# A graph network's edge placement: the weight half of each block's payload products moves from VectorE to GpSimd

## The chip, the core and the metric

The kernel runs on one core of one Trainium2 chip. The metric is the device time of one execution in microseconds, the lower the better; a row of the profile is one instruction or one group of instructions of the engines TensorE (PE, its weight loads PEld), VectorE (DVE), ScalarE (ACT), GpSimd (POOL) and SyncE (SP).

## The reference, cut to what matters

Four graph layers follow each other on 3,125 nodes with 128 features and 53,125 directed edges that are sorted by destination: attention (L0), a sum over neighbours (L1), a layer whose messages carry a weight for each edge (L2), and a relational sum (L3). Only what bears on the change is shown.

```python
loop = arange(3125)
src = concatenate([s, d, loop]); dst = concatenate([d, s, loop])   # then sorted by dst
# L2: a weight for each edge, from its four attributes
e_h = silu(edge_attr @ edge_W1 + edge_b1)
e_w = sigmoid(e_h @ edge_W2 + edge_b2)                             # [53125, 1]
x_agg = silu(x[src] @ agg_W + agg_b) * e_w
out = segment_sum(x_agg, dst) / max(count(dst), 1)
# L0, L1 and L3 use src, dst (and L3 the edge's type) in the same way, without e_w
```

## The kernel before

The nodes are cut into NB = 25 blocks of 128. Before the first layer the kernel sorts the edges into slots: for each block b of destinations and each block j of sources (JN = 26 of them, one for what overflows) there is a tile of 128 slots, and all four layers then work tile by tile with one-hot matrices. This sorting is called placement here. It is a loop over the 25 blocks of destinations. The edges stand in 416 columns of 128, and block b owns a window of CW = 20 columns.

For each block VectorE makes, in this order and each as one instruction: `ohj` (the one-hot of an edge's source block, 20 x 26 bf16 in a partition, line 1578), `LO` (the one-hot of its slot, 128 x 20 bf16, line 1580), and two products at line 1584. A product multiplies `ohj` by three values of each edge and fills half of the payload `PAY` (20 x 3 x 26 = 1,560 bf16 in a partition). Half 0 carries three fields (the offsets of source and destination, the type) and half 1 the edge's weight, split into three bf16 parts. At the end of the block VectorE adds up the three weight parts that came back for the block before (`slot_weights`, line 1546, from PSUM into `EWS`). The values stand in `Wp[:, b, half]`: GpSimd copies them out of the columns, the fields for all blocks at line 837 early on, the weights at line 851 when they are there.

TensorE's `place(b)` (line 2319) multiplies the 20 columns of `LO` by those of `PAY` into a PSUM bank, ScalarE copies the result out (lines 1050 and 1051), and `slot_weights(b)` follows. `ohj`, `LO`, `PAY` and the PSUM bank have two buffers each, taken by b % 2, so VectorE may run up to two blocks ahead of `place`.

The weights come from a small network over the edge attributes, which TensorE and ScalarE compute in pieces (`hidden_piece`: lines 2242, 2255 and 2234 on TensorE, 1031 on ScalarE). They come in two halves. The first is complete before the placement, and serves the blocks 0 to 12 (EARLY = 13). The second is made while blocks 0 to 9 are placed (REST = 10): TensorE's queue holds two `hidden_piece` calls around each `place(n)`, n < 10, and the last of them, the sigmoid and the turned columns come after `place(9)`. Then GpSimd splits the second half into its three parts (lines 844 and 847) and copies the windows of the blocks 13 to 24.

The order of each engine's work is that of the code, engine by engine; between engines there are counting semaphores alone. The ones that matter:

```python
dve.wait_ge(win_ew, b + 1)        # VectorE, ahead of both products: the weights of block b are copied
pool.wait_ge(place_done, NB)      # GpSimd, after its copies: nothing to do until the placement ends
pe.wait_ge(pay_ready, b + 1)      # TensorE, ahead of place(b)
```

After block 24 VectorE compares the first rows of the slots (line 1554), and the first layer begins.

Of the kernel before, what the change touches and what calls it, by code (L numbers as in the profile page):

```python
# [8 lines left out]
ALU = mybir.AluOpType  # L9
# [3 lines left out]
P = 128  # L13
# [31 lines left out]
def gnn_kernel(nc, ins, out):  # L45
    N = ins["x"].shape[0]
    E = ins["src"].shape[0]
    NB = -(-N // P)
# [7 lines left out]
    CW = min(20, NCH)  # L56
# [15 lines left out]
    EARLY = max(0, min(NB, (16 * HA - CW - 4) * P * NB // E + 1))  # L72
    REST = SETS - SB
# [132 lines left out]
    with ctx:  # L206
# [3 lines left out]
        def sem(name):  # L210
            return ctx.enter_context(nc.semaphore(name))
# [56 lines left out]
        PJ = JN // 2  # L268
# [4 lines left out]
        Wp = ring[:, 6240:6240 + 2 * PAYS * NBC].rearrange("p (b w c k t) -> p b w c k t", w=2, c=CW, k=3, t=2)  # L273
# [185 lines left out]
        win_cp = sem("win_cp")  # L459
# [20 lines left out]
        rank_mm = sem("rank_mm")  # L480
        rank_done = sem("rank_done")
        pay_ready = sem("pay_ready")
        place_done = sem("place_done")
        slots_cp = sem("slots_cp")
        ews_done = sem("ews_done")
# [161 lines left out]
        def chunk(n):  # L647
            return adj3[:, n % CBUF, :, :] if n % CBUF < 3 else adj3v[:, n % CBUF - 3, :, :]

        def to_widen(eng, s):  # L650
            n = chunk_of(s)
            eng.wait_ge(adj_io[n % CBUF], adj_stored(n % CBUF) + 16 * (n // CBUF + 1))
            eng.wait_ge(applied, NB * BANKS + max(0, s - XBUF + 1))
            q, b = STEPS[s]
            w = even_width(q)
            return adjf[:, s % XBUF, 0:w], chunk(n)[:, b % ACH, 0:w]

        @block.sync
        def _(sp):
# [155 lines left out]
        def _(pool):  # L815
# [22 lines left out]
            pool.wait_ge(attr_tr, 4)  # L838
            G.tensor_copy(IN, iota_i[:, :].unsqueeze(2).to_broadcast([P, P, CW])).then_inc(pool_consts, 1)

            for h in range(2):
                cs = slice(16 * HALF[h][0], 16 * (HALF[h][-1] + 1))
                pool.wait_ge(ew_act, 3 * h + 2)
                G.tensor_tensor(ewr[:, cs], EW[:, cs], ewp[:, 0, cs], ALU.subtract).then_inc(ew_sub, 1)
                pool.wait_ge(ew_act, 3 * h + 3)
                pool.wait_ge(ew_sub, 2 * h + 1)
                G.tensor_tensor(ewp[:, 2, cs], ewr[:, cs], ewp[:, 1, cs], ALU.subtract).then_inc(ew_sub, 1)
                pool.wait_ge(ew_sub, 2 * h + 2)
                for b in (range(0, EARLY), range(EARLY, NB))[h]:
                    at = pool.value_load(cbi[0:1, b:b + 1], min_val=0, max_val=NCH - CW)  # L850
                    G.tensor_copy(Wp[:, b, 1, :, :, :], ewp[:, :, bass.ds(at, CW)].rearrange("p k c -> p c k").unsqueeze(3).to_broadcast([P, CW, 3, 2])).then_inc(win_ew, 1)

            pool.wait_ge(place_done, NB)
            G.memset(vals[:, :, :, ROW0:VW], 1.0).then_inc(ones_col, 1)
# [524 lines left out]
        def _(dve):  # L1379
# [8 lines left out]
            def loose(instr):  # L1388
                done[0] += 1
                instr.then_inc(dve_order, 1)  # L1390
                return done[0]
# [183 lines left out]
            for b in range(NB):  # L1575
                if b >= 2:
                    dve.wait_ge(place_done, b - 1)
                m = loose(V.tensor_tensor(ohj[:, b % 2, :, :].rearrange("p c (h t) -> p c h t", t=2), IJ2.unsqueeze(1).to_broadcast([P, CW, PJ, 2]),
                                          jr2[:, b, :, :].unsqueeze(2).to_broadcast([P, CW, PJ, 2]), ALU.is_equal))
                loose(V.tensor_tensor(LO[:, b % 2, :, :], IN, lo[:, b, :].unsqueeze(1).to_broadcast([P, P, CW]), ALU.is_equal))  # L1580
                dve.wait_ge(dve_order, m)
                dve.wait_ge(win_ew, b + 1)
                for half in range(2):
                    o = V.tensor_tensor(PAY[:, b % 2, :, 3 * half:3 * half + 3, :].rearrange("p c k (h t) -> p c k h t", t=2),  # L1584
                                        ohj[:, b % 2, :, :].rearrange("p c (h t) -> p c h t", t=2).unsqueeze(2).to_broadcast([P, CW, 3, PJ, 2]),
                                        Wp[:, b, half, :, :, :].unsqueeze(3).to_broadcast([P, CW, 3, PJ, 2]), ALU.mult)
                settle()
                o.then_inc(pay_ready, 1)
                if b:
                    slot_weights(b - 1)  # L1590

            dve.wait_ge(pay_ready, NB)
            for h in FIRST:
                for f in range(2):
                    edge_hots(h, f, 0)
# [607 lines left out]
        def _(pe):  # L2203
# [106 lines left out]

            def place(b):
                pe.wait_ge(pay_ready, b + 1)
                if b >= 2:
                    pe.wait_ge(slots_cp, b - 1)
                    pe.wait_ge(ews_done, b - 1)
                else:
                    pe.wait_ge(rank_done, NB)
                for c in range(CW):
                    o = T.matmul(bank(5 + b % 2)[:, 0:PAYS * JN], LO[:, b % 2, :, c],  # L2319
                                 PAY[:, b % 2, c, :, :].rearrange("p k j -> p (k j)"), start=c == 0, stop=c == CW - 1)  # L2320
                o.then_inc(place_done, 1)
# [429 lines left out]
```

## Time and profile before

| | before |
|---|---|
| median of 3 runs | 1109.53 us (1106.13 to 1110.77) |
| span of the profiled execution | 1106.8 us, 2.7 us under the median |
| placement, from the first `ohj` to the last product | 102.4 to 202.1 us of that span |
| VectorE busy in the placement | 93.73 of 99.80 us |
| TensorE busy in the placement | 85.69 of 99.80 us |
| GpSimd busy in the placement | 24.50 of 99.80 us |

The span reaches from the first to the last instruction of one profiled execution, and all times in the rows below are counted from its start. A measured run is a separate execution. An instruction's duration in a row includes its way in and out of the engine, so that two in a row overlap by some 0.1 us; from start to start is the better measure of what one takes of its engine. GpSimd's durations are rough.

### The profile page before, as it was taken

Reading aid. Unit: us, or ns where it says so; the run is one execution under the profiler, and the core shown is the slowest. Engines: PE = TensorE matmul, PEld = TensorE weight load, DVE = VectorE, ACT = ScalarE, POOL = GpSimd, SP = SyncE. Lnnn points to the kernel's source line nnn. Section 1 sums busy time; section 2 is a strip of 40 time slices with the busy share of each in tenths; the row PEclk is TensorE's granted clock in tenths of the full one; section 3 lists DMA queues with packets and bytes.
Section 4 is the critical chain, followed back from the end, with each engine's and each line's share of the span. In section 5 each row is a group of like instructions: output and inputs, shape, how many; then the busy total and the mean of one; then the engine's idle time right before and its main releaser. Section 6 shows DMA issues by size and latency. Waiting matters only on the chain.

```text
span 1106.8 us, 28220 instructions
## 1 busy us (share of the span) xinstructions
PE 1011.4 (91%) x10463; PEld 867.9 (78%) x10463; DVE 908.4 (82%) x2226; ACT 721.2 (65%) x1559; POOL 219.2 (20%) x260
## 2 busy tenths in 40 slices
PE   3797979699999999995999989779999999999997
PEld 3343557599999999994777777669999999986775
DVE  6775999988998989987988899878787887766754
ACT  3466765555545555547899889677677677776554
POOL 4402240000000000000000000217666667620000
PEclk9899998899999999996999999899999999999998
DMA  6000020345544444412333333234444444457463
GB/s 156 1 1 1 4 67 3 110 144 153 160 137 156 145 155 157 143 46 77 104 125 125 125 112 120 86 110 141 138 135 129 130 139 128 121 185 233 149 169 115
DMA packets 79198, 128.27 MB, mean 116 GB/s; under 512 B 11147, under 2 KB 53206, under 8 KB 78828
## 3 DMA queue, kind: packets, MB, share of 16 engines
q1 hardware_dynamic: 73577, 115.20, 33.5%
q0 software_dynamic: 5056, 10.36, 3.8%
q8 instruction: 87, 1.43, 0.5%
q10 hardware_dynamic: 426, 0.85, 0.3%
q14 instruction: 52, 0.43, 0.1%
HBM read 101.50 MB, written 24.88 MB: 114 GB/s over the span
## 4 chain that ended last, share of the span: by engine, by line
PE 78%; DVE 11%; ACT 5%; issue 3%; DMA 3%; POOL 0%; POOLq 0%; SPq 0%; DVEq 0%; ACTq 0%
PE PS L2416 14%; PE PS L2610 14%; PE PS L2404 11%; PE PS L2593 7%; PE PS L2521 5%; PE PS L2696 5%; PE PS L2489 3%; PE PS L2496 2%; PE PS L2242 2%; PE PS L2255 2%; PE PS L2319 2%; DMA adj_d<-ring 2%; DVE vo L1584 1%; DVE ring L1580 1%; ACT X L1152 1%
## 5 line engine op out<-in xcount | busy, mean ns | idle before, releaser
L1076 ACT CAST vo<-XT 128x768 f32<-128x768 bf16 (+1 forms) x218 | 180.3, 827 | 136.7 <-PE PS L2610 64.1
L912 POOL DMA_INDIRECT XT<-tab,ring x158 | 162.9, 1031 | 109.2 <-PE PS L2610 57.7
L2416 PE MATMUL PS<-vo 128*128 128x133 f32 x1300 | 175.9, 284 | 1.1 <-DVE vo L1686 1.1
L2416 PEld LDWEIGHTS PS<-vo 128*128 128x128 f32 x1300 | 157.2, 191 | 1.2 <-issue 1.2
L2404 PE MATMUL PS<-kp,ring 128*128 128x132 bf16 x1950 | 146.1, 220 | 3.3 <-DVE ring L1554 1.8
L2610 PE MATMUL PS<-vo 128*128 128x128 f32 x984 | 132.8, 279 | 0.0
L2404 PEld LDWEIGHTS PS<-kp,ring 128*128 128x128 bf16 x1950 | 125.3, 97 | 5.5 <-DVE ring L1554 1.9
L1213 ACT CAST ring<-PS 128x512 bf16<-128x512 f32 (+1 forms) x175 | 121.3, 705 | 9.8 <-DMA adj_d<-ring 9.8
L1210 ACT CAST adjf_r<-PS 128x512 fp32r<-128x512 f32 (+1 forms) x175 | 120.3, 698 | 3.6 <-PE PS L2489 3.6
L2610 PEld LDWEIGHTS PS<-vo 128*128 128x128 f32 x984 | 118.9, 191 | 3.0 <-issue 2.4
L1562 DVE TENSOR_TENSOR XT<-iotab,XT 128x768 bf16<-128x768 bf16 (+1 forms) x218 | 119.7, 549 | 1.1 <-ACT XT L1069 1.1
L2406 PE MATMUL PS<-SDP,ring 128*128 128x12 bf16 x650 | 110.1, 169 | 0.0
L1554 DVE TENSOR_SCALAR ring<-ring,pcolm 128x1664 bf16<-128x1664 bf16 x146 | 90.9, 651 | 19.2 <-PE PS L2593 15.5
L2023 DVE TENSOR_TENSOR vo<-PS,EWS 128x640 f32<-128x640 f32 (+2 forms) x109 | 82.4, 756 | 27.4 <-PE PS L2593 27.3
L1686 DVE TENSOR_TENSOR vo<-PS,vo 128x768 f32<-128x768 f32 (+1 forms) x109 | 103.6, 951 | 0.6 <-ACT vo L1126 0.6
L2593 PE MATMUL PS<-kp,ring 128*128 128x128 bf16 x1476 | 99.9, 219 | 0.8 <-ACT big L1232 0.8
L893 POOL IOTA ring<- 128x650 int32 x1 | 0.8, 760 | 495.1 <-PE PS L2496 495.1
L2593 PEld LDWEIGHTS PS<-kp,ring 128*128 128x128 bf16 x1476 | 91.3, 98 | 2.3 <-ACT big L1232 1.0
L1870 DVE TENSOR_TENSOR ring<-IN,SLc 128x512 bf16<-128x512 bf16 x182 | 76.8, 422 | 13.1 <-PE PS L2496 9.3
L2521 PE MATMUL PS<-adjf_r,xh_r 128*128 128x512 f32 (+1 forms) x175 | 80.3, 459 | 1.8 <-ACT adjf_r L1210 1.7
L1126 ACT ACTIVATE vo<-lz,negc 128x24 f32<-128x24 f32 (+1 forms) x109 | 34.7, 318 | 72.4 <-DVE lz L1677 66.6
L2489 PEld LDWEIGHTS PS<-ring 128*128 128x128 bf16 x625 | 43.4, 119 | 47.2 <-issue 28.1
(345 smaller groups left out, 2167.9 us busy)
## 6 DMA issues: line engine op xcount, KB each, us to landing
ring<-rows_d SPq DMA_DIRECT2D x146, 416.0 KB, 4.6
adj_d<-ring SPq DMA_DIRECT2D x100, 128.0 KB, 1.8
adj_d<-ring SPq DMA_DIRECT2D x75, 96.0 KB, 1.7
ring<-adj_d SPq DMA_DIRECT2D x11, 640.0 KB, 4.8
vo<-adj_d SPq DMA_DIRECT2D x9, 640.0 KB, 4.9
vo<-adj_d SPq DMA_DIRECT2D x8, 480.0 KB, 3.9
ring<-adj_d SPq DMA_DIRECT2D x7, 480.0 KB, 4.3
XT<-tab,ring POOLq DMA_INDIRECT x158
```

The costliest lines, as they stand in the source:

```text
L912: G.indirect_dma_start(far_rows[:, f % FBUF, :], None, tab[2], bass.IndirectOffsetOnAxis(ap=far_row[:, t:t + 1], axis=0)).then_inc(far_in[ ...
L1076: C.copy(ohd[:, k % 3, 0:n, :], ohb[:, k % 3, 0:n, :]).then_inc(hots_wide, 1)
L1210: C.copy(adjf[:, s % XBUF, 0:w], bank(s % 3)[:, 0:w]).then_inc(adjf_cp, 1)
L1213: C.copy(adj[:, s % ABUF, 0:w], bank(s % 3)[:, 0:w]).then_inc(adj_cp, 1)
L1562: V.tensor_tensor(ohb[:, k % 3, 0:n, :].rearrange("p t (h d) -> p t h d", d=2), iotab[:, :].rearrange("p (h d) -> p h d", d=2).unsqueeze(1 ...
L1686: V.tensor_tensor(va[:, :, :, 0:F].rearrange("p a i (h f) -> p a i h f", h=H), gathered(k, 0, F).rearrange("p a i (h f) -> p a i h f", h=H ...
L2404: T.matmul(PS[:, to:to + ROW0], ohT[:, 0, h % OBUF, l * P:(l + 1) * P], KP[:, source(t), part, :], start=part == 0, stop=part == 2)
L2406: T.matmul(PS[:, to + ROW0:to + ROW0 + 3 * H], ohT[:, 1, h % OBUF, l * P:(l + 1) * P], SDP[:, t // JN, :, :].rearrange("p t h -> p (t h)") ...
L2416: T.matmul(bank(6 + b % 2)[:, 0:VW], ohd[:, k % 3, i, :], vals[:, k % 3, i, :], start=j == 0, stop=j == JN - 1).then_inc(scattered, 1)
L2521: o = T.matmul(to[:, 0:w], xs[:, b, :], adjf[:, s % XBUF, 0:w], start=b == 0 and part == 0, stop=False, skip_group_check=True)
L2593: o = T.matmul(PS[:, to:to + F], ohT[:, 0, h % OBUF, l * P:(l + 1) * P], XP[:, source(t), part, :], start=part == 0, stop=part == 2)
L2610: T.matmul(bank(6 + q % 2)[:, (b % 4) * P:(b % 4 + 1) * P], rows_of(k, i, t), ohd[:, k % 3, i, :], start=j == 0, stop=j == JN - 1).then_in ...
```

## The change

GpSimd makes the weight half of the product, VectorE the field half. The function `pays(eng, b, half)` holds the product of the old line 1584 for either engine. GpSimd's `weight_pays(b)` waits until the block's weights are copied (`win_ew`), until VectorE has made the block's `ohj` (a new semaphore, `ohj_ready`), and until `place(b - 2)` is through with the buffer. It reports on `pay_weights`, and `place(b)` waits for that and for `pay_ready`. VectorE no longer waits for `win_ew`, but for `pay_weights` of block b - 2 ahead of a new `ohj`.

```diff
+        def pays(eng, b, half):
+            return eng.tensor_tensor(PAY[:, b % 2, :, 3 * half:3 * half + 3, :].rearrange("p c k (h t) -> p c k h t", t=2),
+                                     ohj[:, b % 2, :, :].rearrange("p c (h t) -> p c h t", t=2).unsqueeze(2).to_broadcast([P, CW, 3, PJ, 2]),
+                                     Wp[:, b, half, :, :, :].unsqueeze(3).to_broadcast([P, CW, 3, PJ, 2]), ALU.mult)
...
+            def weight_pays(b):
+                pool.wait_ge(win_ew, b + 1)
+                pool.wait_ge(ohj_ready, b + 1)
+                if b >= 2:
+                    pool.wait_ge(place_done, b - 1)
+                pays(G, b, 1).then_inc(pay_weights, 1)
...
+                if h:
+                    for b in range(min(REST + 1, EARLY), EARLY):
+                        weight_pays(b)
                 for b in (range(0, EARLY), range(EARLY, NB))[h]:
                     at = pool.value_load(cbi[0:1, b:b + 1], min_val=0, max_val=NCH - CW)
                     G.tensor_copy(Wp[:, b, 1, :, :, :], ewp[:, :, bass.ds(at, CW)].rearrange("p k c -> p c k").unsqueeze(3).to_broadcast([P, CW, 3, 2])).then_inc(win_ew, 1)
+                    if h:
+                        weight_pays(b)
+                if h == 0:
+                    for b in range(0, min(REST + 1, EARLY)):
+                        weight_pays(b)
...
                 if b >= 2:
                     dve.wait_ge(place_done, b - 1)
-                m = loose(V.tensor_tensor(ohj[:, b % 2, :, :].rearrange("p c (h t) -> p c h t", t=2), IJ2.unsqueeze(1).to_broadcast([P, CW, PJ, 2]),
-                                          jr2[:, b, :, :].unsqueeze(2).to_broadcast([P, CW, PJ, 2]), ALU.is_equal))
+                    dve.wait_ge(pay_weights, b - 1)
+                V.tensor_tensor(ohj[:, b % 2, :, :].rearrange("p c (h t) -> p c h t", t=2), IJ2.unsqueeze(1).to_broadcast([P, CW, PJ, 2]),
+                                jr2[:, b, :, :].unsqueeze(2).to_broadcast([P, CW, PJ, 2]), ALU.is_equal).then_inc(ohj_ready, 1)
                 loose(V.tensor_tensor(LO[:, b % 2, :, :], IN, lo[:, b, :].unsqueeze(1).to_broadcast([P, P, CW]), ALU.is_equal))
-                dve.wait_ge(dve_order, m)
-                dve.wait_ge(win_ew, b + 1)
-                for half in range(2):
-                    o = V.tensor_tensor(PAY[:, b % 2, :, 3 * half:3 * half + 3, :].rearrange("p c k (h t) -> p c k h t", t=2),
...
+                dve.wait_ge(ohj_ready, b + 1)
+                dve.wait_ge(win_cp, NB)
                 settle()
-                o.then_inc(pay_ready, 1)
+                pays(V, b, 0).then_inc(pay_ready, 1)
                 if b:
                     slot_weights(b - 1)
 
             dve.wait_ge(pay_ready, NB)
+            dve.wait_ge(pay_weights, NB)
...
                 pe.wait_ge(pay_ready, b + 1)
+                pe.wait_ge(pay_weights, b + 1)
```

GpSimd's queue at the end of the first half of the weights, before: the last copy of a window, then the split of the second half. `ring` holds `Wp`, `big` the weights, `cbi` the windows' first columns.

```order
L850 TENSOR_LOAD cbi
L850 ISA x2
L851 ISA
L851 COPY ring<-big 128x120
L844 TENSOR_TENSOR big<-EW,big 128x192 [waits ew_act]
L847 TENSOR_TENSOR big<-big 128x192 [waits ew_sub,ew_act]
L850 TENSOR_LOAD cbi [waits ew_sub]
L850 ISA x2
L851 ISA
L851 COPY ring<-big 128x120
```

The same place in the change, where `vo` holds `PAY` (the line numbers are those of the changed file).

```order
L868 COPY ring<-big 128x120
L661 TENSOR_TENSOR vo<-big,ring 128x20x78 [waits ohj_ready,win_ew] x2
L661 TENSOR_TENSOR vo<-big,ring 128x20x78 [waits place_done,ohj_ready,win_ew] x9
L858 TENSOR_TENSOR big<-EW,big 128x192 [waits ew_act]
L861 TENSOR_TENSOR big<-big 128x192 [waits ew_sub,ew_act]
L661 TENSOR_TENSOR vo<-big,ring 128x20x78 [waits ohj_ready,place_done,win_ew,ew_sub]
L661 TENSOR_TENSOR vo<-big,ring 128x20x78 [waits place_done,ohj_ready,win_ew]
L867 TENSOR_LOAD cbi
L867 ISA x2
L868 ISA
L868 COPY ring<-big 128x120
L661 TENSOR_TENSOR vo<-big,ring 128x20x78 [waits place_done,ohj_ready,win_ew]
```

Eleven products (blocks 0 to 10) now stand between the copies of the first half and the split of the second, two (blocks 11 and 12) behind the split, and one behind each copy of the second half.

VectorE's queue for one block in the middle of the loop, before.

```order
L1578 TENSOR_TENSOR big<-IJ,ring 128x520 [waits place_done]
L1580 TENSOR_TENSOR ring<-big,lo 128x2560
L1584 TENSOR_TENSOR vo<-big,ring 128x20x78 [waits win_ew,dve_order]
L1584 TENSOR_TENSOR vo<-big,ring 128x20x78
L1546 TENSOR_REDUCE EWS<-PS 128x26 [waits slots_cp,dve_order]
```

The same block in the change.

```order
L1601 TENSOR_TENSOR big<-IJ,ring 128x520 [waits pay_weights,place_done]
L1603 TENSOR_TENSOR ring<-big,lo 128x2560
L661 TENSOR_TENSOR vo<-big,ring 128x20x78 [waits dve_order,win_cp,ohj_ready]
L1568 TENSOR_REDUCE EWS<-PS 128x26 [waits slots_cp]
L1601 TENSOR_TENSOR big<-IJ,ring 128x520 [waits pay_weights,place_done]
```

One of the two products is gone from VectorE's queue, and `ohj` waits for GpSimd's product of two blocks before.

## Rows read from the trace of the kernel before

**Rows 1.** The page, its first line: the span of the profiled execution.

```profile
span 1106.8 us, 28220 instructions
```

**Rows 2.** Busy time in three windows: us, engines, TensorE's granted clock, DMA.

```profile
102.40:202.20 99.80, 85.69 (x785) 59.85 (x781) 93.73 (x124) 62.56 (x165) 24.50 (x29) 0.93 0.08 21
161.00:164.00 3.00, 1.32 (x19) 1.17 (x17) 3.00 (x3) 0.98 (x4) 3.00 (x4) 1.00 0.01 2
164.00:168.00 4.00, 3.59 (x25) 3.05 (x25) 4.00 (x7) 0.60 (x2) 0.50 (x1) 0.65 0.06 12
```

**Rows 3.** Chain that ended last, 172 to 204 us: shares, and its last TensorE piece.

```profile
by line: DVE ring L1580 35.0%; DVE vo L1584 32.6%; issue 10.7%; DVE big L1578 8.7%; PE PS L2319 5.5%; DVE EWS L1546 4.7%; ACT SLc L1051 1.6%; ACT SLr L1050 0.9%; DVEq L1582 0.4%; DVEq L1544 0.1%; DVEq L1549 0.1%
...
202.19 1.62 PE PS L2319 x20
```

**Rows 4.** Timeline of VectorE, one late block: start, duration, instruction.

```profile
187.45 0.23 DVE L1546 TENSOR_REDUCE EWS<-PS 128x26 f32<-128x78 f32 x1
187.60 0.42 DVE L1578 TENSOR_TENSOR big<-IJ,ring 128x520 bf16<-128x520 bf16 x1
187.93 1.49 DVE L1580 TENSOR_TENSOR ring<-big,lo 128x2560 bf16<-128x2560 bf16 x1
189.34 1.85 DVE L1584 TENSOR_TENSOR vo<-big,ring 128x1560 bf16<-128x1560 bf16 x2
191.10 0.23 DVE L1546 TENSOR_REDUCE EWS<-PS 128x26 f32<-128x78 f32 x1
```

**Rows 5.** Timeline of VectorE and GpSimd at 33, 40 and 103 us.

```profile
33.29 1.89 DVE L1519 TENSOR_TENSOR big<-big 128x1664 bf16<-128x1664 f32 x1
33.35 1.91 POOL L836 COPY ring<-big 128x40 bf16 x1
...
39.77 2.31 POOL L839 CAST big<-iota_i 128x2560 bf16<-128x2560 int32 x1
...
40.05 2.08 DVE L1468 TENSOR_TENSOR ring<-ring 128x60 bf16<-128x60 bf16 x1
...
102.63 0.64 POOL L844 TENSOR_TENSOR big<-EW,big 128x224 f32<-128x224 f32 x1 [60.54 <-ACT big L1019]
...
102.72 1.90 DVE L1580 TENSOR_TENSOR ring<-big,lo 128x2560 bf16<-128x2560 bf16 x1
...
103.75 1.33 POOL L847 TENSOR_TENSOR big<-big 128x224 bf16<-128x224 f32 x1 [0.49 <-ACT big L1021]
```

**Rows 6.** Timeline of GpSimd: copies at 22 us and from 105.8 us.

```profile
22.72 0.28 POOL L837 COPY ring<-big 128x120 bf16 x1
22.95 0.21 POOL L836 COPY ring<-big 128x40 bf16 x1
...
105.80 0.28 POOL L851 COPY ring<-big 128x120 bf16 x1 [0.73 <-POOL big L847]
106.48 10.01 POOL L851 COPY ring<-big 128x120 bf16 x12 [0.40 <-issue]
```

**Rows 7.** Timeline of GpSimd: its products of two tensors with VectorE idle.

```profile
150.68 0.56 POOL L844 TENSOR_TENSOR big<-EW,big 128x192 f32<-128x192 f32 x1 [34.19 <-ACT big L1019]
151.70 0.55 POOL L847 TENSOR_TENSOR big<-big 128x192 bf16<-128x192 f32 x1 [0.46 <-ACT big L1021]
...
700.92 1.33 POOL L899 TENSOR_TENSOR ring<-ring,SLr 128x650 f32<-128x650 f32 x1
```

**Rows 8.** Timeline of TensorE and VectorE around the blocks 0, 3, 4 and 9.

```profile
108.19 2.82 PE L2319 MATMUL PS<-vo,ring 128*128 128x156 bf16 x20 [4.94 <-DVE vo L1584]
...
111.90 0.23 DVE L1546 TENSOR_REDUCE EWS<-PS 128x26 f32<-128x78 f32 x1
...
119.55 0.59 PE L2242 MATMUL PS<-big,We1b 99*128 99x512 bf16 x2
...
123.24 0.59 PE L2242 MATMUL PS<-big,We1b 99*128 99x512 bf16 x2
...
143.85 1.55 PE L2319 MATMUL PS<-vo,ring 128*128 128x156 bf16 x20
```

More of the change, by code:

```diff
@@ L482, in gnn_kernel @@
         pay_ready = sem("pay_ready")
+        pay_weights = sem("pay_weights")
+        ohj_ready = sem("ohj_ready")
         place_done = sem("place_done")
@@ L1577, in _ @@
                     dve.wait_ge(place_done, b - 1)
-                m = loose(V.tensor_tensor(ohj[:, b % 2, :, :].rearrange("p c (h t) -> p c h t", t=2), IJ2.unsqueeze(1).to_broadcast([P, CW, PJ, 2]),
-                                          jr2[:, b, :, :].unsqueeze(2).to_broadcast([P, CW, PJ, 2]), ALU.is_equal))
+                    dve.wait_ge(pay_weights, b - 1)
+                V.tensor_tensor(ohj[:, b % 2, :, :].rearrange("p c (h t) -> p c h t", t=2), IJ2.unsqueeze(1).to_broadcast([P, CW, PJ, 2]),
+                                jr2[:, b, :, :].unsqueeze(2).to_broadcast([P, CW, PJ, 2]), ALU.is_equal).then_inc(ohj_ready, 1)
                 loose(V.tensor_tensor(LO[:, b % 2, :, :], IN, lo[:, b, :].unsqueeze(1).to_broadcast([P, P, CW]), ALU.is_equal))
-                dve.wait_ge(dve_order, m)
-                dve.wait_ge(win_ew, b + 1)
-                for half in range(2):
-                    o = V.tensor_tensor(PAY[:, b % 2, :, 3 * half:3 * half + 3, :].rearrange("p c k (h t) -> p c k h t", t=2),
-                                        ohj[:, b % 2, :, :].rearrange("p c (h t) -> p c h t", t=2).unsqueeze(2).to_broadcast([P, CW, 3, PJ, 2]),
-                                        Wp[:, b, half, :, :, :].unsqueeze(3).to_broadcast([P, CW, 3, PJ, 2]), ALU.mult)
+                dve.wait_ge(ohj_ready, b + 1)
+                dve.wait_ge(win_cp, NB)
                 settle()
-                o.then_inc(pay_ready, 1)
+                pays(V, b, 0).then_inc(pay_ready, 1)
                 if b:
```

## The prediction

> **What bounds the kernel now.** I read the span first [rows 1], then the busy time in the stretch of the placement, then the chain of waits inside it, then single instructions in the timeline. Between 102.4 and 202.2 us VectorE is busy for 93.73 of 99.80 us, more than TensorE (85.69), and GpSimd for 24.50 [rows 2]. The chain of waits over the second part of this stretch is nearly all VectorE's: `LO`, the two products, `ohj` and the sum of `slot_weights` stand in it one after another, and TensorE comes in with 5.5% [rows 3]. So a late block costs what VectorE needs for it. From one `slot_weights` to the next that is 191.10 - 187.45 = 3.65 us: 0.15 for the sum, 0.33 for `ohj`, 1.41 for `LO`, 1.76 for the two products, each from start to start [rows 4], so 0.88 for one product. In the first ten blocks TensorE is as tight: its queue turns over in 123.24 - 119.55 = 3.69 us for each block [rows 8]. The placement ends at about 202.1 us, where the last `place` begins [rows 3].
>
> **What the change does.** It takes 25 products of 0.88 us from VectorE and gives 25 of the same shape to GpSimd. Were the two engines independent and GpSimd fast, a block would cost VectorE 2.77 us, and 22 us could be gained at most. Two questions decide: how long GpSimd takes for one product, and whether VectorE can work meanwhile.
>
> **Can both work at once?** Three places show the two engines excluding each other [rows 5]. At 33.35 a GpSimd copy of 40 elements takes 1.91 us and ends at 35.26; VectorE's two-tensor instruction that began at 33.29 ends at 35.18. At 39.77 a GpSimd cast takes 2.31 us, to 42.08; a VectorE instruction of 60 elements that began inside it takes 2.08, to 42.13, where `ohj` with 520 takes 0.42 [rows 4]. And at 102.72 it is the very pair of the change: `LO` began while GpSimd's subtraction ran to 103.27, and lasted 1.90 instead of 1.49, to 104.62; GpSimd's next subtraction, begun at 103.75, lasted 1.33, to 105.08, so only 0.46 after `LO` had ended. In each case the later instruction waits for the whole of the earlier one and then needs its own time. `ohj`, `LO` and the field product read two tensors from SBUF as these did; the sum of `slot_weights` reads PSUM and is not of the kind. I therefore take it that GpSimd's product shuts VectorE out for its full length, and that VectorE's saving is 0.88 us a block while its new stall is GpSimd's whole product.
>
> **How long is GpSimd's product?** The trace has none of this shape. With VectorE idle a two-tensor instruction took 0.555 us for 192 elements and 1.33 for 650 [rows 7]. The line through both, 1.69 ns an element beyond 650, gives 1.33 + 910 x 1.69 / 1000 = 2.87 us for 1,560. The time of an element in the longer row, start-up included (2.04 ns), gives 3.19. That of the shorter row (2.89 ns) gives 4.51. I take 3.2, since 650 elements are nearest to 1,560, and keep 2.87 and 4.51 as bounds; that these rows are fp32 and the product bf16 with repeated operands I can't price.
>
> The Trainium skill, GPSIMD Engine Reference, section 3.1, gives 4497 ns for a GpSimd addition of 2,048 fp32 elements, against 2293 on VectorE. Scaled to 1,560 elements that would be an estimate of 3.43 us, and the sum below would come out some 6 us later. The rows of this trace are used instead.
>
> **The sum.** A block costs 3.65 - 0.88 + 3.2 = 5.97 us, if what GpSimd waits for is there. Step by step against the profiled execution:
>
> GpSimd's 13 copies of windows begin at 105.80 as before. VectorE no longer waits for them, runs through the blocks 0 and 1 (`LO` ends at 104.62, the field product follows GpSimd's subtraction at 105.08, then `ohj`, `LO` and a product, 2.6 us more) and is out of work at about 108.6. Until then one copy gets in after each of its four instructions; before, 12 copies against a busy VectorE took 10.01 us. The other nine follow at 0.23 us each, the distance of the free copies [rows 6]. GpSimd's first product so begins at 111.0. It ends at 114.2, the second at 117.4. `place(0)` begins at 114.2 instead of 108.19; with its 2.82 us and the 0.9 from there to `slot_weights(0)` [rows 8], `ohj` of block 2 begins at 118.05. Block 2 is complete at 118.05 + 0.33 + 1.41 + 3.2 + 0.88 = 123.9, and block 9 at 123.9 + 7 x 5.97 = 165.7.
>
> The second half of the weights hangs on `place(9)`: before, it began at 143.85, GpSimd's split at 150.68, and 1.6 us later the parts were there [rows 7, 8]. Now that is 165.7 + 6.83 + 1.6 = 174.1, some 0.5 us later than GpSimd could take block 11. So block 11 is complete at 123.9 + 9 x 5.97 + 0.5 = 178.1. The last 13 blocks each have a copy besides; a copy that gets in between two VectorE instructions costs it little, and I put 0.1 us. Block 24 is complete at 178.1 + 13 x 6.07 = 257.0, against 202.1: 55 us later. What follows begins as before, so I forecast 1109.53 + 55 = 1164 us. On the profile's own span, 2.7 us below the median, it is 1162.
>
> With 2.87 us for the product the same steps give +47 (1156), with 4.51 they give +87 (1196). The added waits cost nothing of their own beside this. `ohj` now waits for GpSimd's product of two blocks before, with `LO` and the field product queued behind it; that product is done a block earlier, since VectorE can't pass it. `place` waits for `pay_weights`, with the `hidden_piece` calls behind it; it takes 1.55 us in the tight part and 2.82 in block 0, after TensorE had been idle [rows 8], against 5.97 for a block. Behind GpSimd's first eleven products stands the split of the second half, which is the 0.5 us above. Were GpSimd quick, each wait would show with a semaphore's delay. No transfer is moved.
>
> **Rivals.** *They overlap.* If GpSimd's bf16 product did not shut VectorE out, the block would cost the slower of 2.77 us on VectorE, 3.69 on TensorE (first ten blocks) and GpSimd's product with its copy. Blocks 0 to 9 would then keep TensorE's 3.69 but start some 5.7 us later, since the 13 copies stand ahead of the first product: `place(9)` at 149.6, the parts at 158.0. Fourteen products and 12 copies of 0.23 follow. At 2.87 us that ends at 201.0, a gain of 1 us: 1108. It decides at 2.95 us a product; at 2.5 it would be 6 us faster, at 4.51, where blocks 0 to 9 take GpSimd's pace, 28 slower. For it speaks only that no row has a bf16 product on GpSimd; against it stand all three places of [rows 5]. Chance 0.12, of which 0.03 faster, 0.07 the same, 0.02 slower.
>
> The Trainium skill, Perfetto Trace Analysis, section Optimizing Scalar/DVE Operations, holds that giving work of a saturated VectorE to GpSimd can make sense, and adds that it might not help, because the two share a read port. Its first half is this rival; the trace shows the second.
>
> *GpSimd is slower than its rows.* Inner runs of two elements and two repeated operands may cost it more: up to 4.51 us, 1173 to 1196. Chance 0.13. The copies of rows 6 have such runs and show no extra, but have one operand.
>
> *TensorE falls to half its clock.* It stands idle for 2.3 us of each block where it had none. The granted clock was 1.00 in 161 to 164 us, where it was busy for 1.32 of 3.00, and 0.65 in the 4 us after that [rows 2], so in part at the lower level. Were it at 1.2 instead of 2.4 GHz throughout, the 3.69 us of a block would become up to 7.4, which is 1.4 over the 5.97: for blocks 2 to 9 another 11 us, 1175. Chance 0.10; over the whole placement, with its idle and its busy blocks, the granted clock is 0.93 [rows 2].
>
> **How the numbers follow.** The forecast, the two engines in turn with 2.8 to 3.5 us a product (1154 to 1173), has 0.65. With the slower product and the lower clock 0.88 lies above 1150, and 0.02 more where they overlap but GpSimd is slow: slower 0.90, same 0.07, faster 0.03, where "same" is within 0.5% (5.5 us), about what runs of this kernel can tell from no change. The range 1148 to 1190 leaves out the overlap and the longest products; its lower end also allows 8 us that the hand-overs may hide: the subtraction that waited behind `LO` needed 0.46 us for 224 elements, the free one 0.55 for 192 [rows 5, 7], so part of an instruction's start-up can pass while it waits.
>
> **What would show it.** GpSimd's line of the product: 25 instructions, about 3.2 us of work each, longer in the record where it waits behind `LO`. VectorE's field product: about 4 us in the record instead of 0.96, as it waits inside. From one `slot_weights` to the next about 6 us; the end of the placement near 257 us; everything after it shifted, not changed. If VectorE's three instructions keep 0.42, 1.49 and 0.96 us next to GpSimd's product, the exclusion is wrong. If the block takes less than 5.5 or more than 7.3 us, the product's price is.

## The result, and the profile after

The changed kernel takes 1157.98 us (median of 4 runs, 1155.76 to 1162.24), the kernel before on the same chip 1110.15 (4 runs): a ratio of 1.0438, 95% interval 1.0414 to 1.0462, so 47.8 us slower. The profiled execution is the longest of the four (1162.24 us). The first line of its page answers to [rows 1]:

```profile
span 1160.3 us, 28268 instructions
```

Timeline of VectorE and GpSimd, one block in the middle of the loop; it answers to [rows 4]. L1601 is `ohj`, L1603 `LO`, L661 the product on either engine, L1568 `slot_weights`.

```profile
128.16 0.23 DVE L1568 TENSOR_REDUCE EWS<-PS 128x26 f32<-128x78 f32 x1
128.31 0.41 DVE L1601 TENSOR_TENSOR big<-IJ,ring 128x520 bf16<-128x520 bf16 x1
128.65 1.48 DVE L1603 TENSOR_TENSOR ring<-big,lo 128x2560 bf16<-128x2560 bf16 x1
128.86 3.95 POOL L661 TENSOR_TENSOR vo<-big,ring 128x1560 bf16<-128x1560 bf16 x1 [1.45 <-DVE big L1601]
130.26 3.38 DVE L661 TENSOR_TENSOR vo<-big,ring 128x1560 bf16<-128x1560 bf16 x1
133.56 0.23 DVE L1568 TENSOR_REDUCE EWS<-PS 128x26 f32<-128x78 f32 x1
...
244.46 3.38 DVE L661 TENSOR_TENSOR vo<-big,ring 128x1560 bf16<-128x1560 bf16 x1
247.76 0.23 DVE L1568 TENSOR_REDUCE EWS<-PS 128x26 f32<-128x78 f32 x1
```

Read it from start to start. GpSimd's product is released by `ohj` and begins in the record at 128.86, 0.21 after `LO` has begun. It ends at 132.81. VectorE's product is in the record from 130.26, right behind `LO`, and lasts 3.38 us where it needs 0.88 [rows 4]: it ends 0.83 after GpSimd's. So the three run one after another: `LO`, GpSimd's product, VectorE's product. VectorE looks busy all the time and is not; its "busy" product is mostly a wait. The block takes 133.56 - 128.16 = 5.40 us instead of 3.65. Take away VectorE's own 2.77, and GpSimd's product costs 2.63 in its turn.

The beginning of the placement on GpSimd, which answers to the second part of [rows 6] (the copies are at L868 here, the splits at L858 and L861):

```profile
108.07 0.28 POOL L868 COPY ring<-big 128x120 bf16 x1 [0.72 <-POOL big L861]
108.75 3.09 POOL L868 COPY ring<-big 128x120 bf16 x5 [0.40 <-issue]
...
115.44 0.29 POOL L868 COPY ring<-big 128x120 bf16 x1 [0.38 <-issue]
116.11 0.29 POOL L868 COPY ring<-big 128x120 bf16 x1 [0.39 <-issue]
116.36 5.61 POOL L661 TENSOR_TENSOR vo<-big,ring 128x1560 bf16<-128x1560 bf16 x2
```

The free copies are 0.67 us apart, though each is only 0.29 long: 0.38 passes in issuing. Two products run one behind the other with VectorE idle, 2.8 us each: that is the free price. VectorE has nothing to do until `slot_weights(0)`, 11.5 us. The timeline of VectorE at the end of that gap and behind the placement:

```profile
122.75 0.24 DVE L1568 TENSOR_REDUCE EWS<-PS 128x26 f32<-128x78 f32 x1 [11.51 <-ACT SLc L1073]
...
256.86 0.28 DVE L1633 TENSOR_REDUCE exc<-PS 16x1 f32<-16x128 f32 x1 [3.95 <-PE PS L2443]
```

The last row is the reduction into `exc`, the first thing in which VectorE waits for TensorE after the placement. It comes 9.1 us after the last `slot_weights` row above, with a wait of 3.95. In the kernel before, the same two rows are 5.8 us apart, with a wait of 0.68:

```profile
202.05 0.23 DVE L1546 TENSOR_REDUCE EWS<-PS 128x26 f32<-128x78 f32 x1
...
207.88 0.28 DVE L1613 TENSOR_REDUCE exc<-PS 16x1 f32<-16x128 f32 x1 [0.68 <-PE PS L2422]
```

The windows of the changed kernel (columns as in [rows 2]) show why:

```profile
126.00:172.00 46.00, 34.44 (x317) 18.65 (x316) 44.93 (x36) 28.12 (x63) 33.04 (x9) 1.00 0.01 2
...
248.00:258.00 10.00, 8.54 (x78) 7.86 (x78) 5.24 (x17) 1.47 (x6) 0.13 (x1) 0.57 0.29 69
```

TensorE keeps the full clock (1.00, 2.4 GHz) through the blocks 2 to 9, although it idles in each. In the later blocks it does not (0.85 from 200 to 230 us), but they take 5.40 us all the same. Behind the placement it is granted 0.57, near the lower level of 1.2 GHz. The last `place` and the first layer's gather, which stand in TensorE's queue ahead of the transposition that feeds `exc`, then take longer: the last `place` 2.82 us (the line below) where it took 1.62 before [rows 3].

```profile
247.90 2.82 PE L2340 MATMUL PS<-vo,ring 128*128 128x156 bf16 x20 [2.50 <-DVE vo L661]
```

Before, the window around the same work (202 to 208) reads 1.00:

```profile
202.00:208.00 6.00, 4.66 (x74) 4.23 (x74) 5.14 (x18) 1.88 (x7) 0.13 (x1) 1.00 0.06 12
```

So the time went here: from 102.37 to 202.05 the placement took 99.7 us, from 104.64 to 247.76 it took 143.1, which is 43.4 more; 3.3 more pass until `exc`. The profiled execution also began its placement 2.3 us later and lost some 4.5 us in the later stages (below). Together that is the 53.5 us between the two spans; the medians differ by less, as the profiled execution is 4.3 us above its median.

### The profile page after: what moved, and what is told of

Same layout as the page of the kernel before. It is cut to its first block, busy times and chain, and to the rows that moved or that the text cites. A ratio compares the mean times of both kernels' runs of the same rounds, so it can differ in the third digit from the quotient of the medians.

```text
span 1160.3 us, 28268 instructions
## 1 busy us (share of the span) xinstructions
PE 1028.5 (89%) x10463; PEld 880.1 (76%) x10463; DVE 943.6 (81%) x2201; ACT 722.8 (62%) x1559; POOL 309.7 (27%) x285
## 4 chain that ended last, share of the span: by engine, by line
PE 72%; DVE 13%; issue 7%; ACT 4%; DMA 3%; SPq 0%; POOLq 0%; DVEq 0%; POOL 0%; ACTq 0%
PE PS L2437 13%; PE PS L2631 13%; PE PS L2425 11%; PE PS L2614 7%; PE PS L2542 6%; PE PS L2717 5%; PE PS L2510 3%; DVE ring L1603 3%; PE PS L2517 2%; DVE vo L661 2%; DMA adj_d<-ring 2%; PE PS L2275 1%; PE PS L2262 1%; ACT X L1174 1%; DVE big L1601 1%
## 5 line engine op out<-in xcount | busy, mean ns | idle before, releaser
L2425 PE MATMUL PS<-kp,ring 128*128 128x132 bf16 x1950 | 148.5, 222 | 3.3 <-DVE ring L1576 1.8
L1235 ACT CAST ring<-PS 128x512 bf16<-128x512 f32 (+1 forms) x175 | 115.3, 665 | 10.1 <-DMA adj_d<-ring 10.0
L1232 ACT CAST adjf_r<-PS 128x512 fp32r<-128x512 f32 (+1 forms) x175 | 114.5, 660 | 5.4 <-PE PS L2510 5.3
L661 POOL TENSOR_TENSOR vo<-big,ring 128x1560 bf16<-128x1560 bf16 x25 | 95.4, 3816 | 19.3 <-DVE big L1601 13.1
L2340 PE MATMUL PS<-vo,ring 128*128 128x156 bf16 x500 | 49.3, 265 | 44.1 <-DVE vo L661 29.8
```

The costliest lines, as they stand in the source:

```text
L661: return eng.tensor_tensor(PAY[:, b % 2, :, 3 * half:3 * half + 3, :].rearrange("p c k (h t) -> p c k h t", t=2), ohj[:, b % 2, :, :].rear ...
L1232: C.copy(adjf[:, s % XBUF, 0:w], bank(s % 3)[:, 0:w]).then_inc(adjf_cp, 1)
L1235: C.copy(adj[:, s % ABUF, 0:w], bank(s % 3)[:, 0:w]).then_inc(adj_cp, 1)
L2425: T.matmul(PS[:, to:to + ROW0], ohT[:, 0, h % OBUF, l * P:(l + 1) * P], KP[:, source(t), part, :], start=part == 0, stop=part == 2)
```

## The experiments

All twelve in one table, with the two kernels of the case. "Late block" is from one `slot_weights` to the next in the second half of the placement; "exc" is the start of the reduction into `exc`; "rest" is the span less that start. These three come from one profiled execution of each kernel; the ratio is to runs of the kernel before on the same chip.

| kernel | median us | ratio (95%) | late block | exc | rest |
|---|---|---|---|---|---|
| before | 1110.15 | | 3.65 | 207.9 | 898.9 |
| the change | 1157.98 | 1.0438 (1.0414 to 1.0462) | 5.40 | 256.9 | 903.4 |
| e1_spare_product | 1177.41 | 1.061 (1.0583 to 1.0637) | 6.37 | 273.5 | 902.8 |
| e2_spare_memset | 1116.4 | 1.006 (1.0042 to 1.0078) | 3.98 | 210.9 | 902.8 |
| e3_spare_copy | 1163.53 | 1.0485 (1.0451 to 1.0519) | 5.86 | 259.0 | 900.6 |
| e4_six_columns | 1129.77 | 1.0185 (1.0161 to 1.021) | 4.27 | 225.9 | 904.3 |
| e5_copies_between | 1154.38 | 1.0395 (1.0366 to 1.0424) | 5.40 | 247.1 | 906.8 |
| e6_filled | 1155.89 | 1.0418 (1.0392 to 1.0444) | 5.40 | 251.3 | 907.6 |
| e7_back_on_dve | 1115.28 | 1.0059 (1.004 to 1.0078) | 3.87 | 211.2 | 904.1 |
| e8_no_weights | 1100.46 | 0.993 (0.9908 to 0.9953) | 2.98 to 3.56 | 197.2 | 900.4 |
| e9_wait_ahead | 1115.76 | 1.0069 (1.0055 to 1.0083) | 3.87 | 209.8 | 900.8 |
| e10_wait_behind | 1109.77 | 1.0014 (1.0003 to 1.0026) | 3.65 | 206.2 | 901.5 |
| e11_one_product | 1111.07 | 1.0022 (1.0012 to 1.0032) | 3.58 | 206.5 | 903.5 |
| e12_before_again | 1109.01 | 0.9989 (0.9974 to 1.0004) | 3.65 | 208.0 | 898.9 |

**Do the engines exclude each other, and by what?** Theory: the two engines take turns at SBUF, by the operands that are read. Rival: VectorE waits for GpSimd's results, by the semaphores of the change. Three kernels leave the computation of before as it is and give GpSimd one spare instruction a block, whose result nobody reads: a product of the change's shape, a fill of 3,120 elements, a copy of 2,560.

```diff
+            def spare_work(b):
+                if b:
+                    pool.wait_ge(pay_ready, b)
+                    pool.wait_ge(spare_done, b)
+                G.memset(spare, 0.0).then_inc(spare_done, 1)
```

This is e2. In e1 the last line is a product as in the change, of 520 elements of `IN` (the constant that `LO` is compared with) and the field values of block b; in e3 it is a copy of 2,560 elements of `IN`.

> The kernel before, and besides one GpSimd product a block of the same shape and types as the one of the change (1,560 bf16, two tensors read from SBUF), written to a spare place that nothing in the placement waits for. Theory (the engines exclude each other while both read two tensors from SBUF): a late block takes 3.65 + 2.65 = 6.3 us, VectorE's instruction that meets the product lasts 2.6 us longer, and some 21 blocks so give +56, 1166 us. Rival (the change is slow because VectorE and TensorE wait by semaphore for a slow GpSimd): nobody waits here, a block stays at 3.65 us and the time at 1110.

> As the spare product, but GpSimd only writes: a memset of 3,120 bf16, by the memset of 2,184 in the trace (1.91 us) about 2.7 us. If what excludes is the reading of SBUF, a late block stays at 3.65 to 3.7 us and the time at 1110 to 1112. If any work of GpSimd excludes VectorE, a block takes 3.65 + 2.6 = 6.3 us and the time is about 1165.

> As the spare product, but GpSimd copies 2,560 bf16, so reads one tensor; by the cast of 2,560 in the trace (2.31 us) about 2.2 us. If one tensor read by GpSimd is enough to exclude VectorE's two-tensor instructions, a late block takes 3.65 + 2.15 = 5.8 us and the time is about 1155. If GpSimd must read two, it stays at 3.65 us and 1110.

Timeline of e1_spare_product around the second half's split and in a late block (GpSimd's spare product is L847, `ohj` L1597, `LO` L1599, both products of before L1603):

```profile
178.47 6.41 POOL L847 TENSOR_TENSOR vo<-big,ring 128x1560 bf16<-128x1560 bf16 x2
179.15 0.23 DVE L1565 TENSOR_REDUCE EWS<-PS 128x26 f32<-128x78 f32 x1
179.29 2.90 DVE L1597 TENSOR_TENSOR big<-IJ,ring 128x520 bf16<-128x520 bf16 x1
...
188.16 3.10 POOL L847 TENSOR_TENSOR vo<-big,ring 128x1560 bf16<-128x1560 bf16 x1 [1.79 <-DVE vo L1603]
188.49 4.11 DVE L1599 TENSOR_TENSOR ring<-big,lo 128x2560 bf16<-128x2560 bf16 x1
```

`LO` needs nothing from GpSimd here, and still it lasts 4.11 us. At 179.15 the sum from PSUM passes through in its usual 0.23 us inside GpSimd's product, and the `ohj` behind it takes 2.90. The same part of e3_spare_copy:

```profile
181.88 2.60 POOL L847 COPY vo<-big 128x2560 bf16<-128x2560 bf16 x1 [1.76 <-DVE vo L1601]
181.88 0.41 DVE L1595 TENSOR_TENSOR big<-IJ,ring 128x520 bf16<-128x520 bf16 x1
182.22 3.60 DVE L1597 TENSOR_TENSOR ring<-big,lo 128x2560 bf16<-128x2560 bf16 x1
```

One operand read by GpSimd is enough. And e2_spare_memset, where GpSimd reads nothing, early on and in a late block:

```profile
117.96 22.41 POOL L847 MEMSET vo<- 128x3120 bf16 x8
123.44 0.41 DVE L1595 TENSOR_TENSOR big<-IJ,ring 128x520 bf16<-128x520 bf16 x1
123.78 1.48 DVE L1597 TENSOR_TENSOR ring<-big,lo 128x2560 bf16<-128x2560 bf16 x1
125.18 1.84 DVE L1601 TENSOR_TENSOR vo<-big,ring 128x1560 bf16<-128x1560 bf16 x2
...
168.84 2.69 POOL L847 MEMSET vo<- 128x3120 bf16 x1
169.00 1.85 DVE L1601 TENSOR_TENSOR vo<-big,ring 128x1560 bf16<-128x1560 bf16 x2 [0.25 <-POOL ring L862]
```

Early on eight fills run without a gap, and `ohj`, `LO` and the two products inside them keep their 0.41, 1.48 and 1.84 us. In the late block the two products keep their 1.85 us next to a fill of 2.69. The 0.25 ahead of them is another thing: GpSimd's copy of the window (L862) now stands behind its fill, the two take 3.98 us, and VectorE waits for the copy. The theory holds and the rival falls. The Trainium skill, SBUF — State Buffer, section Who interferes with whom, says that a VectorE instruction with two SBUF inputs contends with a GpSimd instruction that reads SBUF, and not with one that only writes it; the 3.60 and the 1.48 to 1.85 above agree. The times were expected too low. e1 was expected 56 us longer than the kernel before, and its profiled execution is 69.5 us longer: 62.3 up to the last `slot_weights` of the loop (264.4), 3.3 between there and `exc` as in the change, and 3.9 in the rest. e2 is in the placement only 0.6 us longer than the first profile of before; 2.4 us lie between there and `exc`, and 3.9 in the rest.

**What an element costs.** The change with GpSimd making only 6 of the 20 columns of the weight half (468 elements), VectorE the other 14.

```diff
...
-                pays(G, b, 1).then_inc(pay_weights, 1)
+                pays(G, b, 1, 0, 6).then_inc(pay_weights, 1)
...
-                pays(V, b, 0).then_inc(pay_ready, 1)
+                pays(V, b, 0)
+                dve.wait_ge(win_ew, b + 1)
+                pays(V, b, 1, 6, CW).then_inc(pay_ready, 1)
```

> The change, but GpSimd makes only 6 of the 20 columns of the weight half (468 elements) and VectorE the other 14 behind its field half. Theory (exclusion): GpSimd's part costs 0.3 x 2.63 = 0.79 us of VectorE's time where VectorE's own would have cost 0.3 x 0.88: a late block takes 3.65 - 0.88 + 0.67 + 0.79 = 4.2 us, the first product starts as late as in the change, and the time is about 1130. Rival (GpSimd's length is the pace and VectorE is free beside it): 0.8 us fit into the block, a late block takes 3.4 us, and the time is 1105 to 1117.

Timeline, one late block and the free pair at the start:

```profile
114.63 1.91 POOL L662 TENSOR_TENSOR vo<-big,ring 128x468 bf16<-128x468 bf16 x2
...
175.00 0.23 DVE L1569 TENSOR_REDUCE EWS<-PS 128x26 f32<-128x78 f32 x1
...
175.69 2.11 POOL L662 TENSOR_TENSOR vo<-big,ring 128x468 bf16<-128x468 bf16 x1 [1.20 <-issue]
177.10 2.25 DVE L662 TENSOR_TENSOR vo<-big,ring 128x1560 bf16<-128x1560 bf16 x2
...
179.27 0.23 DVE L1569 TENSOR_REDUCE EWS<-PS 128x26 f32<-128x78 f32 x1
```

The theory holds here too: the block takes 4.27 us, the median is 1129.77, and the rival's 3.4 us fell. If VectorE's part shrinks with its columns, its share of the block is 2.77 + 0.88 x 14/20 = 3.39, so 468 elements cost 0.88 in their turn. With 2.63 for 1,560 that is (2.63 - 0.88) / 1092 = 1.60 ns an element and 0.13 us for the instruction. VectorE pays 0.88 us for 1,560, or 0.56 ns each. As long as the two take turns, every element that is moved loses about 1 ns. By these prices no split is a gain; only this one and the whole half were run.

**The start.** In the change 13 copies stand ahead of the first product. Here each of the first eleven products follows its own copy.

```diff
-                    if h:
-                        weight_pays(b)
-                if h == 0:
-                    for b in range(0, min(REST + 1, EARLY)):
+                    if h or b < REST + 1:
                         weight_pays(b)
```

> The change, but in the first half each copy of a window stands right ahead of its block's product instead of all 13 ahead of the first. Theory (the change loses some 8 us at its start, where the copies of 0.67 us hold the first product back to 116.4 us of its profile, and later copies fall between VectorE's instructions for nothing): the first product begins near 108.4 us, blocks stay at 5.40 us, and the time is 1150 to 1152. Rival (the copies would have to be paid somewhere anyway): within 3 us of the change's 1158.

The first product begins at 106.33 instead of 116.36 and the last `slot_weights` of the loop stands at 240.10. The placement, from the first `ohj` at 102.53, takes 137.6 us instead of 143.1. From the same start of the placement 7.9 us are won there and 5.5 are left: at the second half's split VectorE waits 1.59 us for ScalarE's copy of the slots, where the change has 0.36, and the first blocks with their copies in between are a little longer. In the profile `exc` also follows 2.1 us sooner on the last `slot_weights`, and the rest is 3.4 us longer than in the change. The median is 3.6 us lower; it lies between the two expectations.

**TensorE's clock behind the placement.** 28 idle matmuls ahead of each `place(b)`, b >= 13, into a bank that nobody reads.

```diff
             def place(b):
+                if b >= EARLY:
+                    for _ in range(28):
+                        T.matmul(bank(4)[:, 0:P], onesb[:, :], onesb[:, :], start=True, stop=True)
```

> The change, with 28 matmuls of 128 columns, whose result nobody reads, ahead of each place from block 13 on. Theory (the 3.3 us that the change loses between the last product and the first layer are TensorE's lower granted clock, which follows from its idle time in each block): the granted clock right after the placement is near 1.00 instead of 0.57, the stretch from the last product to the reduction behind it (line 1633) shrinks from 9.1 to about 6 us, blocks stay at 5.40 us, and the time falls by about 3 us to 1155. Rival (something else holds that stretch): it stays at 9 us.

Its windows:

```profile
230.00:246.00 16.00, 12.58 (x165) 10.93 (x164) 15.60 (x12) 6.57 (x20) 13.79 (x5) 1.00 0.02 5
246.00:256.00 10.00, 5.36 (x81) 4.72 (x78) 8.04 (x32) 2.25 (x7) 0.13 (x1) 0.94 0.26 74
256.00:262.00 6.00, 4.05 (x29) 3.91 (x30) 5.34 (x14) 4.42 (x10) 0.00 (x0) 0.50 0.80 286
```

With TensorE busy for 12.58 of 16.00 us the clock stays at 1.00, and from the last `slot_weights` (245.51) to `exc` (251.33) it is 5.8 us again. So the 3.3 us are the clock's. But it then falls to 0.50 right behind, and the median gains 2 us at most, which these runs can't tell from none. The lower clock does not need the longer block. e7 and e9 (below) both have late blocks of 3.87 us; behind the placement e7 (first line) is granted 0.55 and takes 8.1 us to `exc`, e9 (second line) 1.00 and 5.8:

```profile
206.50:212.00 5.50, 4.87 (x52) 4.57 (x51) 2.26 (x8) 0.50 (x2) 0.00 (x0) 0.55 0.41 120
...
204.00:210.00 6.00, 4.66 (x74) 4.23 (x74) 5.15 (x18) 1.59 (x7) 0.13 (x1) 1.00 0.08 14
```

What makes the difference between these two stays open.

**The waits of the change alone.** e7 is the change with both products back on VectorE, so that only its new semaphores and the new places of its waits are left.

> The change with all its semaphores and waits, but VectorE makes the weight half too, right behind the field half. Theory (the new waits are free, GpSimd's product is the whole cost): a late block takes 3.65 to 3.7 us and the time is that of the kernel before, 1108 to 1113. Rival (the waits and the two-step hand-over to TensorE cost something themselves): 0.2 us or more a block, 1115 and above.

The theory that the waits are free fell: 1115.28 us, and a late block of 3.87. The timeline of e7_back_on_dve:

```profile
172.67 1.48 DVE L1599 TENSOR_TENSOR ring<-big,lo 128x2560 bf16<-128x2560 bf16 x1
174.28 1.85 DVE L661 TENSOR_TENSOR vo<-big,ring 128x1560 bf16<-128x1560 bf16 x2
```

From `LO` to the product it is 1.61 us, where [rows 4] have 1.41: VectorE waits for the end of its own `LO`, since `settle()` stands ahead of the product now and behind both before. e9 makes that edit alone in the kernel before (the first diff), e10 undoes it in e7 (the second).

```diff
+                settle()
                 for half in range(2):
...
-                settle()
                 o.then_inc(pay_ready, 1)
```

```diff
-                settle()
                 pays(V, b, 0).then_inc(pay_ready, 1)
                 dve.wait_ge(win_ew, b + 1)
-                pays(V, b, 1).then_inc(pay_weights, 1)
+                o = pays(V, b, 1)
+                settle()
+                o.then_inc(pay_weights, 1)
```

> The kernel before, with one line moved: VectorE's wait for its own LO stands ahead of the two products instead of behind them. Theory (the 0.22 us a block that was lost where both products were back on VectorE is this wait): a late block takes 3.87 us instead of 3.65, 25 blocks some 5.5 us, 1113 to 1116 us in all against 1108.7 for the kernel before. Rival (it is one of the other waits of the change, such as TensorE's for two semaphores instead of one): 1108 to 1110, late block 3.65 us.

> The change with both products back on VectorE, and the wait for LO behind the products, as in the kernel before. Theory: the late block is back at 3.65 us and the time at 1108 to 1110. Rival (another wait of the change costs it): the late block stays at 3.87 us and the time at 1114 to 1116.

Late blocks of 3.87 and 3.65 us, medians of 1115.76 and 1109.77: what the late block loses is this one wait, and the new semaphores, which e10 keeps, cost next to nothing (1.0014). That the medians differ by 6 us is not fully explained. e9's profiled execution, the fastest of its six, has `exc` 1.9 us later than the first profile of before, and its rest is 1.9 us longer. Its first ten blocks also take 3.87 us where before they take 3.7, but the wait for the second half is shorter in return (5.56 us from one `slot_weights` to the next, against 6.16). Where the other 3 us of e9's median lie no profile shows. In the change itself the wait costs nothing: GpSimd's product runs to 132.81 in the timeline above, and VectorE's, in the record from 130.26, waits for it in any case.

**What there was to win.** e8 leaves the weight half out: nobody makes it, and the edges' weights come out as zero. It is the change with a GpSimd that takes no time and waits for no weights; VectorE's wait for its own `LO` is still ahead of the product. e11 joins the two products of before into one instruction.

> Nobody makes the weight half: that half of the payload is set to zero once, so all edge weights come out as zero. This is what an entirely free GpSimd would give. If VectorE were the only bound, each of 25 blocks would be 0.88 us shorter and the time 1088. My theory: TensorE is right behind with 3.69 us a block in the first ten and about 3.5 in the late ones with their keys, so the gain is only the 2.4 us stall at block 11 and 0.1 to 0.3 us a late block: 1100 to 1107.

> The kernel before, with the two products of a block made as one instruction of 3,120 elements (the weights' layout changed to suit). Theory: only the way in and out of one instruction is saved, below 0.1 us of a late block's 3.65, so about 1 us over the 13 late blocks and nothing in the first ten, where TensorE takes 3.69 us a block: 1106 to 1109. Rival: the inner dimensions cost VectorE more in one instruction, late block above 3.65 and the time above 1110.

e8 gains 8 us, not 22. Its window over the first ten blocks:

```profile
119.00:143.00 24.00, 24.00 (x236) 13.59 (x233) 19.13 (x28) 19.92 (x47) 0.00 (x0) 1.00 0.02 4
```

TensorE is busy for all 24.00 us and turns a block over in 3.69, as before. The late blocks take 2.98 to 3.56; in the longer ones VectorE waits for ScalarE's copy of the slots, as the timeline of e8_no_weights has it:

```profile
174.46 0.24 DVE L1565 TENSOR_REDUCE EWS<-PS 128x26 f32<-128x78 f32 x1 [0.48 <-ACT SLc L1070]
...
177.91 0.24 DVE L1565 TENSOR_REDUCE EWS<-PS 128x26 f32<-128x78 f32 x1 [0.36 <-ACT SLc L1070]
```

e11 shortens the late block to 3.58, as its theory had it, but its median is 2.4 above the kernel before, which the theory had not; its placement of 98.3 us lies between the two of before (97.5 and 99.7, see below). No version here that computes the weights beats the kernel before.

**The rest.** In every other kernel the part behind `exc` is 1.5 to 8.7 us longer than in the first profile of before, though its instructions are the same.

> The kernel before, unchanged, timed and profiled as if it were an experiment. In its first profile the part behind the placement (from the first TENSOR_REDUCE of exc to the end) took 898.9 us; in the profiles of the other kernels of this study, whose instructions there are the same, it took 900.4 to 907.6 us. Theory (it is the scatter of runs): here it takes between 900 and 907 us too, and the ratio is 1.000 within 0.002. Rival (the other kernels make that part longer): it takes 897 to 900 us, as in the first profile, and the ratio is again 1.000.

898.9 us once more, as the rival has it. That does not rule scatter out. Each rest is that of one execution: both profiles of before are of about the same length (spans of 1106.8 and 1106.9 us), while the measured runs of this kernel reach from 1105.5 to 1113.9 us, and the two profiles with rests of 903.4 (the change) and 907.6 (e6) are 4.3 and 4.8 us above their kernels' medians. Most of the difference in the profiles lies in the building of the adjacency in the second layer (from its first product with the features to the third layer's first gather 225.8 us in both profiles of before, 229.9 in the change, 233.1 in e6), where TensorE, VectorE and ScalarE wait for each other and for transfers in many short pieces. Whether it differs from kernel to kernel or from run to run, and why, stays open. Differences of medians of some 5 us are therefore not put down to the placement here unless the placement's own rows show them. e12 also began its placement 2.2 us later than the first profile (at 104.6) and ended it at the same time (202.1): it has not the 1.3 us that one block lost there (167.92 to 172.84, against 3.65), and was 0.9 quicker over the first ten. So the placement of before takes 97.5 to 99.7 us; that of the change takes 143.1 from either start (104.64 to 247.76, and in e6 102.4 to 245.5).

## Why the prediction was right

**The exclusion held.** "GpSimd's product shuts VectorE out for its full length" is what the block shows, and e1 and e3 show it without any wait of VectorE for GpSimd's spare instruction. e2 limits it: its fill, which only writes, shuts nothing out. The rival of overlap fell.

**The product was mis-sized.** The block of 5.40 us lies just under the 5.5 that the prediction named as the sign of that. The step was "I take 3.2, since 650 elements are nearest to 1,560". It is 2.8 us free and 2.63 in its turn. The line through both rows of [rows 7] gave 2.87: the longer row's mean time of an element counted its start-up once more for each 650 elements. That 2.63 is 0.2 below 2.8 fits with the start-up passing in part while GpSimd waits, as the lower end of the prediction's range allowed; no experiment tests it. 22 blocks of 5.40 instead of 5.97 are 12.5 us less. The rival of a slower product fell with it; the Trainium skill's figure in the prediction (GPSIMD Engine Reference, section 3.1), scaled to 3.43 us, is further off.

**The copies** were taken at 0.23 us each, "the distance of the free copies". These, free as well, came 0.67 apart. The copies of [rows 6] at 22 us stood behind one that had been held up, and a little earlier the same loop shows in the kernel before what an undisturbed turn of two copies takes: 0.80 us, with 0.34 of it in issuing.

```profile
20.12 0.22 POOL L836 COPY ring<-big 128x40 bf16 x1 [0.34 <-issue]
20.28 0.29 POOL L837 COPY ring<-big 128x120 bf16 x1
20.92 1.46 POOL L836 COPY ring<-big 128x40 bf16 x1 [0.35 <-issue]
```

So the distance was read from the wrong rows, and the first product, counted from the same start of the placement, came 3.1 us later than said. The two free products gave back 0.8 of it, and block 2 was complete 2.0 late. The 0.1 us for each late copy was nothing, as a late block is 5.39 to 5.40 like the others: 1.3 us less. The hand-over at block 11 cost 0.8 instead of 0.5.

**Together**: 257.0 + 2.0 - 12.5 - 1.3 + 0.3 = 245.5, and with the profile's later start 247.8, where it ended.

**TensorE's clock** was a rival for blocks 2 to 9 and did not fall there. "What follows begins as before" is the step that failed by its side: behind the placement the clock was at 0.57, 3.3 us. With 43.4 in the placement (45.6 against the 97.5 of e12) that is 46.7 to 48.9 us, and the medians differ by 47.8. The forecast of 1164 us is near the measured 1158 partly by luck: in the placement it was 11.5 us too high, and 3.3 of that were hidden by the clock, which it had put at nothing.

**"22 us could be gained at most"** was too kind: e8 shows 8, since TensorE's pace in the first ten blocks and, in part of the late ones, ScalarE's copy come next.

## What to carry to other kernels

Before work moves from a busy VectorE to an idle GpSimd, look for two instructions of the two engines that meet in the trace: where both read SBUF and VectorE's has two operands there, expect the move to be worth the difference of their prices, here 0.56 against 1.60 ns an element, a loss. An engine whose busy share stays high may be waiting inside its instructions: compare an instruction's duration with the same one alone. And before pricing a gain, take the work out altogether once, as e8 does; what is left is set by the next engine.

## What was not expected of the hardware

- A GpSimd copy with a single operand shuts VectorE's two-operand instruction out (3.60 us instead of 1.48); a fill of about the same length (2.69 us against the copy's 2.60) does not, and VectorE's sum from PSUM passes through in 0.23 us.
- An instruction of VectorE that waits for the end of the one before it begins about 0.2 us later than one that follows without a wait (1.61 against 1.41 us from `LO` to the product).
- Free GpSimd copies whose place is read from a register came 0.67 us apart at 0.29 us each, while some that stood behind a held one came 0.23 apart.
- A placement in which TensorE is busy for 10.6 of the last 18 us was followed by a granted clock of 0.57, and by 0.94 where it had been kept busy for 12.6 of 16, with 0.50 soon after. Behind two kernels with equal late blocks, e7 and e9, it was 0.55 and 1.00.
